# Four transformer layers and a routed expert layer on one core: joining the masks of two block pairs, moving bulk loads into the loop, preparing the experts' second group earlier

## The reference

```python
x = x + attn(layernorm(x))     # 4 layers inside
x = x + ffn(layernorm(x))      # experts
# attn: for each of 4 layers, h being the running state
xn = ln(h); q, k, v = xn @ Wq.T + bq, xn @ Wk.T + bk, xn @ Wv.T + bv     # 16 heads of 8
rel = einsum('bhqd,ld->bhql', q + u, pos_emb)
scores = (q k^T + rel_shift(rel)) * 8**-0.5; scores = where(k > q, NEG, scores)
h = h + softmax(scores) v @ Wo.T + bo
h = h + gelu(ln(h) @ W1.T + b1) @ W2.T + b2                              # 128 -> 512 -> 128
# ffn: a shared gated unit of width 256, and 16 experts of width 32
shared = silu(x @ sg.T) * (x @ su.T) @ sd.T
combine = weights of the top 4 of 16 experts, from the 2 best of 4 groups
routed = sum over e of (silu(x @ g_e) * (x @ u_e) * combine_e) @ d_e
```

## Time and profile before

| | |
|---|---|
| runs | 2417.66, 2413.36, 2417.36 us, median 2417.36 |
| profiled execution | 2418.66 us; its span 2416.9 us |
| granted TensorE clock, mean | 0.985 of full |
| instructions | 83238 |

### The profile page before, as it was taken

How to read it: one execution, slowest core, us unless ns; L and a number is a source line. 1 busy time by engine, 2 the same in 40 slices (tenths; PEclk the granted TensorE clock), 3 DMA queues, 4 the chain that set the end, 5 groups by cost and what they waited for, 6 DMA issues and landing times. The chain is left out here.

```text
span 2416.9 us, 83238 instructions
## 1 busy us (share of the span) xinstructions
PE 2301.1 (95%) x31360; PEld 1983.0 (82%) x31360; DVE 2020.7 (84%) x5071; ACT 1832.1 (76%) x2869; POOL 1145.7 (47%) x2089
## 2 busy tenths in 40 slices
PE   3899999999999999999999999999999999799998
PEld 2788888888888888888888888888888887577776
DVE  6899999888888888888888888888888885577774
ACT  2588888888888888888888888888878888455554
POOL 4355555455555544545555555454445543233332
PEclk9899999999999999999999999999999999699999
DMA  6333333333333333333333333333333330000000
GB/s 195 91 81 88 95 88 88 85 87 89 90 91 96 91 89 88 90 92 82 90 89 95 90 92 91 91 85 91 92 95 91 91 92 26 24 27 27 27 23 18
DMA packets 221160, 196.05 MB, mean 81 GB/s; under 512 B 28896, under 2 KB 217440, under 8 KB 220768
## 3 DMA queue, kind: packets, MB, share of 16 engines
q1 hardware_dynamic: 220768, 190.73, 29.2%
HBM read 14.46 MB, written 4.19 MB: 8 GB/s over the span
## 5 line engine op out<-in xcount | busy, mean ns | idle before, releaser
L961 DVE TENSOR_REDUCE rowmax<-bank 128x4 f32<-128x1024 f32 (+1 forms) x768 | 914.2, 1218 | 108.5 <-PE bank L556 96.4
L766 ACT ACTIVATE probs<-bank 128x1024 f32<-128x1024 f32 x768 | 745.7, 1024 | 89.2 <-PE bank L613 77.1
L613 PE MATMUL bank<-qstack,kstack 64*128 64x128 f32 (+1 forms) x4096 | 433.3, 304 | 0.0
L556 PE MATMUL bank<-kstack,qstack 62*128 62x256 f32 (+1 forms) x4096 | 427.1, 305 | 0.0
L807 ACT ACT_TABLE_LOAD x256 | 328.4, 1283 | 4.5
L556 PEld LDWEIGHTS bank<-kstack,qstack 62*128 62x128 f32 x4096 | 315.6, 193 | 0.0
L613 PEld LDWEIGHTS bank<-qstack,kstack 64*128 64x128 f32 x4096 | 314.8, 191 | 0.0
L545 PE MATMUL bank<-mask_half,pick_half 64*128 64x128 bf16 (+1 forms) x3072 | 269.6, 243 | 16.1 <-DMA qstack<-base 13.7
L602 PE MATMUL bank<-maskT_half,pick_half 64*128 64x128 bf16 (+1 forms) x3072 | 268.8, 241 | 15.2 <-DVE rowmax L961 10.5
L698 PE MATMUL bank<-w,hidden 128*128 128x128 f32 x2048 | 274.6, 278 | 2.6 <-ACT hidden L816 2.6
L633 PE MATMUL bank<-probs,v_pad 128*32 128x256 f32 x4096 | 271.1, 382 | 0.6 <-DVE v_tok L942 0.6
(11 more groups left out here) (151 smaller groups left out, 5261.8 us busy)
## 6 DMA issues: line engine op xcount, KB each, us to landing
qstack<-base SPq DMA_DIRECT2D x768, 128.0 KB, 2.4
kstack<-base SPq DMA_DIRECT2D x384, 128.0 KB, 2.5
turn_x<-turn_c SPq DMA_DIRECT2D x512, 32.0 KB, 1.8
qstack<-maxrows SPq DMA_DIRECT2D x256, 16.0 KB
out<-ot SPq DMA_DIRECT2D x16, 256.0 KB, 2.4
xin<-in_x SPq DMA_DIRECT2D x15, 256.0 KB, 3.1
w<-in_w SPq DMA_DIRECT2D x4, 256.0 KB, 3.1
w_in<-in_w_in SPq DMA_DIRECT2D x1, 768.0 KB, 4.3
```

What stands on the lines that cost most here:

```text
L556: last = pe.matmul(bank[:, b0 + b, i * wide:(i + 1) * wide], qstack[rows, r, p0 + i, t * 128:(t + 1) * 128], kstack[rows, r, p0 + i, 0:wid ...
L613: last = pe.matmul(bank[:, b0 + b, i * wide:(i + 1) * wide], kstack[rows, r, p0 + i, kt * 128:(kt + 1) * 128], qstack[rows, r, p0 + i, q0: ...
L766: act.activation(probs[:, k], bank[:, A_BANK[k]:A_BANK[k] + 2, :], ACT.Exp, scale=SCALE).then_inc(exp_done[k], 1)
L961: dve.tensor_reduce(rowmax[:, n % 2, t, :, p0:p0 + heads], bank[:, M_BANK[k]:M_BANK[k] + 2, :].rearrange("p b (h c) -> p b h c", h=heads), ...
```

## The change

Four things are moved; no product and no transfer is added or dropped, but the second group's residual now reads its x through `turn`, a tile that no one uses any more by then.

1. **Masks.** `m_round` is split into `m_masks` and `m_scores`, `a_round` into `a_masks` and `a_scores`. For most rounds they are called one after the other. At two places of a slot, a1 with m2 and m5 with a0, both masks come first and both sets of scores behind them. The wait of m5 for its stacks and of a5 for `maxrows` now stands at the scores.
2. **Bulk loads.** They move from SP's start into slots, each behind `exchange`: x rows 3 in slot 1, b_o, w_1, w_o in slot 2, b_2, b_1, w_2 in slot 3, x rows 4 and 5 in slots 4 and 8, w_qkv of layers 1 to 3 in slot 10. POOL splits `w_1` in slot 3 instead of slot 1.
3. **POOL in the drain.** The power of the experts' group 0 moves from the end of slot 131 to slot 132, behind `xn2_split`.
4. **Second group.** Its x is loaded in slot 129, its residual and statistics are made by DVE in slot 132, its power by POOL in slot 133, its norm as the first thing of DVE in the slots of the expert part (`norm(1)`).

```diff
@@ sync
-            sp.dma_start(w_1[:], a["w_1"][0]).then_inc(w1_landed, 16)
-            sp.dma_start(b_o[:], on_all("bo")).then_inc(later_landed, 16)
...
-            for c in range(3, len(X_STARTS)):
-                rows_of_x(c)
-            sp.dma_start(w_qkv[:, 1:LAYERS], a["w_qkv"].rearrange("l p n -> p l n")[:, 1:LAYERS]).then_inc(later_landed, 16)
+
+            def loads_behind(s):
+
+                if s == 1:
+                    rows_of_x(3)
+                if s == 2:
+                    sp.dma_start(b_o[:], on_all("bo")).then_inc(later_landed, 16)
+                    sp.dma_start(w_1[:], a["w_1"][0]).then_inc(w1_landed, 16)
+                    sp.dma_start(w_o[:], a["w_o"].rearrange("l p n -> p l n")).then_inc(later_landed, 16)
+                if s == 3:
...
+                    sp.dma_start(w_2[:], a["w_2"].rearrange("l (c p) n -> p l c n", p=128)).then_inc(later_landed, 16)
+                if s in (4, 8):
+                    rows_of_x(3 + s // 4)
+                if s == 10:
+                    sp.dma_start(w_qkv[:, 1:LAYERS], a["w_qkv"].rearrange("l p n -> p l n")[:, 1:LAYERS]
+                                 ).then_inc(w_rest_landed, 16)
+            def experts_second():
+
+                sp.wait_ge(cosines_used, N)
+                sp.dma_start(turn[:].rearrange("p b (t d) -> p b t d", t=T), x_tiles[:, GT // T:2 * GT // T]
+                             ).then_inc(ex.second_landed, 16)
@@ tensor, the slot's order
-                    a_round(s - 4, 1)
+                    a_masks(s - 4, 1)
                 if live(s - 2):
-                    m_round(s - 2, 2)
+                    m_masks(s - 2, 2)
                 if live(s - 4):
-                    a_round(s - 4, 4)
+                    a_scores(s - 4, 1)
                 if live(s - 2):
-                    m_round(s - 2, 1)
+                    m_scores(s - 2, 2)
...
                 if live(s - 1):
-                    m_round(s - 1, 5)
+                    m_masks(s - 1, 5)
                 if live(s - 3):
-                    a_round(s - 3, 0)
+                    a_masks(s - 3, 0)
+                if live(s - 1):
+                    m_scores(s - 1, 5)
                 if live(s - 3):
-                    a_round(s - 3, 3)
+                    a_scores(s - 3, 0)
@@ vector
+            def experts_stats_second():
+                h = h_all[:, 2:4].rearrange("p b t d -> p (b t) d")
+                dve.wait_ge(ex.second_landed, 16)
+                dve.wait_ge(h2_ready, N - B + 4)
+                dve.tensor_tensor(h, turn[:].rearrange("p b (t d) -> p (b t) d", t=T), h, ALU.add).then_inc(ex.x1_ready, 1)
...
                 if s == N + 4:
                     experts_norm()
+                    experts_stats_second()
@@ gpsimd
+                if s in (N + 4, N + 5):
+                    g = s - N - 3
+                    pool.wait_ge(ex.mv_ready, g)
+                    pool.tensor_scalar(ex.ve[:], ex.mv[:, :, 1], 1e-5, None, ALU.add).then_inc(ex.ve_ready, 1)
+                    pool.wait_ge(ex.ve_ready, g)
+                    at_least(pool, ex.xn_ready, g - 1)
+                    pool.tensor_tensor(ex.rstd[:], ex.ve[:], expo[:, 0:GT], ALU.pow).then_inc(ex.rstd_ready, 1)
...
-                if s == N + 3:
-                    pool.wait_ge(ex.mv_ready, 1)
@@ experts, vector
-                    if u == 1 and live(q + 2) and q + 2 > 0:
+                    if u == 1 and live(q + 2) and q + 2 > 1:
                         residual(q + 2, v + 2)
...
+            norm(1)
             slots(dve, slot)
```

More of the change, by code:

```diff
@@ L179 @@
     landed: object
+    second_landed: object
     x1_ready: object
@@ L513, in values, with m_mask, m_masks @@
                 last.then_inc(v_done, 1)
[L515 to L520, removed]
+            def m_mask(k, half):
+                heads = 4 if k < 2 else 2
+                for b in range(TILES):
+                    rows = slice(b * ROWS, (b + 1) * ROWS)
+                    v = bank[:, M_BANK[k] + b, :].rearrange("p (h k) -> p h k", h=heads)
+                    c = (0 if k < 2 else 128) + half * 64
+                    pe.matmul(v[:, :, c:c + 64], pick_half[rows, half], mask_half[rows, half, 0:heads],
+                              start=(half == 0), stop=True, skip_group_check=True)
+            def m_masks(n, k):
                 if k == 0:
@@ L536, in m_round, with m_scores @@
                     bank_left(pe, (live(n - 3), context_out, n - 2), (live(n + 1), v_ready, n + 2))
+                m_mask(k, 0)
+                if k >= 2:
+                    m_mask(k, 1)
+            def m_scores(n, k):
+                r, b0 = n % RING, M_BANK[k]
+                if k == M_FIRST:
+                    pe.wait_ge(stack_landed[r], 16 * STACK_DMAS * (n // RING + 1))
+                    pe.wait_ge(rot_landed[r], 16 * NP * (n // RING + 1))
                 t, heads = (0, 4) if k < 2 else (1, 2)
                 p0, wide = heads * (k - 2 * t), 512 // heads
[L540 to L550 removed]
                 for i in range(heads):
                     if heads == 4 and i == 1:
[L553 removed]
+                        m_mask(k, 1)
                     for b in range(TILES):
@@ L569, in m1, with a_mask, a_masks @@
                 last.then_inc(max_turned, 1)
-            def a_round(n, k):
-                r, b0 = n % RING, A_BANK[k]
-                if k == A_FIRST:
-                    pe.wait_ge(maxrows_landed, 32 * (n + 1))
+            def a_mask(k, half):
+                heads = 2 if k % 3 < 2 else 4
+                for b in range(TILES):
+                    rows = slice(b * ROWS, (b + 1) * ROWS)
+                    v = bank[:, A_BANK[k] + b, :].rearrange("p (h q) -> p h q", h=heads)
+                    c = half * 64
+                    pe.matmul(v[:, :, c:c + 64], pick_half[rows, 2 + half], maskT_half[rows, half, 0:heads],
+                              start=(half == 0), stop=True, skip_group_check=True)
+            def a_masks(n, k):
                 if k == 0:
@@ L595, in a_round @@
                 p0, wide = 4 * half + (2 * kind if kind < 2 else 0), 512 // heads
-                def mask(part):
-                    for b in range(TILES):
-                        rows = slice(b * ROWS, (b + 1) * ROWS)
-                        v = bank[:, b0 + b, :].rearrange("p (h q) -> p h q", h=heads)
-                        c = part * 64
-                        pe.matmul(v[:, :, c:c + 64], pick_half[rows, 2 + part], maskT_half[rows, part, 0:heads],
-                                  start=(part == 0), stop=True, skip_group_check=True)
-                mask(0)
-                if heads == 2:
-                    mask(1)
                 for i in range(heads):
                     if heads == 4 and i == 1:
-                        mask(1)
+                        a_mask(k, 1)
                     for b in range(TILES):
@@ L1330, in load @@
                     sp.dma_start(xin[:, v % 2], x_groups[q]).then_inc(xin_landed[v % 2], 16)
-            load(1, 1)
             def slot(q, v):
```

84 lines of the change are left out of this document (56 added, 28 removed).

## The result

The changed kernel takes 2404.88 us, the median of 5 runs (2402.57 to 2405.32), against 2417.25 us (5 runs) for the kernel before on the same chip: a ratio of 0.9949, 95% interval 0.9938 to 0.9961. I had predicted 2401.5 us. The profiled executions are 2418.66 and 2404.88 us with spans of 2416.9 and 2403.1: 13.8 us came in where I had summed 15.8. The joins, the drain and the expert part brought more than worked out, and the start had the wrong sign. That these offset each other is luck, and without it the sum would have been far off.

What follows compares the result with a forecast made beforehand. A slot was bound by a cycle of PE stretches and waits for DVE's maxima. Terms 6.2 + 2.0 + 2.7 + 4.9 = 15.8 us off 2418.66 gave 2402.9, less 1.3 to the median: 2401.5 us, range 2391 to 2411.

Steps and rivals of the forecast that it cites:

- Joined masks: In the slots: joining a1 and m2 saves 0.05 us in about 124 slots, 6.2 us; joining m5 and a0 saves 0.
- a2 waiting for the delayed exponential: In the slot, ahead of the wait at `f2`: a2's mask may wait up to 0.1 us; counted as nothing.
- The start, first half: At the start: with the loads moved away, the first exchange and content come sooner, 7.0 us saved.
- The start, second half: In slots 1 to 10: the six moved loads cost 5.0 us, leaving 2.0 us of the start's gain.
- The rate: Bulk loads in the slots: at 238 GB/s 1.05 MB of x takes 4.4 us, part of it while SP issues.
- The room: Before `split_first`: 3.0 us to spare in slot 8; no feed-forward hangs on ACT in slots 1 to 4.
- The sign that I had named: In slots 4 to 10: the clock falling behind a load would show the prediction wrong; no size given.
- the far bound: For one moved load in the slots: the worst row, `experts_early`, lost 5.0 us; bounds were 0 and 5.0.
- The drain: In slot 132: POOL splits item 126 ahead of the experts' power, so the split comes 2.7 us sooner.
- the clock comes back sooner: Rival for drain and expert part: products leave the half clock level earlier, 8 us more, 2393.5 us; chance 0.16.
- The expert part: At the second `x_turn`: PE's wait for the second group's norm goes away, 4.9 us saved.
- slower, each load costs 5.0: Rival for the moved loads: late stacks hold ACT and the clock falls, 30 us instead of 5, 2426.5 us; chance 0.05.

Runs made afterwards that it cites:

- no_joins: The changed kernel with both joins taken apart, each round's masks right ahead of its scores again: 2415.19 us, ratio 0.9998 to the kernel before the change.
- m2_scores_first: m2's scores put ahead of a1's, against the changed kernel with bulk and early loads ahead of the exchange (2388.59 us): 2400.26 us.
- before: The kernel without the change, against which the ratios are taken: 2417.25 us beside the changed kernel.
- after: The changed kernel as profiled, with all four moves, against the kernel without them: 2404.88 us, ratio 0.9949.
- loads_on_act_queue: The changed kernel with the bulk loads of slots 1, 2, 3, 4, 8 and 10 issued by ACT on its own queue instead of SP: 2392.98 us.
- pool_order_old: The changed kernel with the power of the experts' group 0 back at slot 131's end on POOL, ahead of item 126's split: 2410.64 us.
- second_group_old: The changed kernel with the second group's x, residual, statistics and norm back in the expert part: 2408.72 us, ratio 0.9977.
- loads_at_start: The changed kernel with its bulk loads back at the start of SP's queue, ahead of the first exchange: 2398.13 us, ratio 0.9921.

## Why the prediction was nearly right in sum and wrong in a term

- **Joined masks: right, 7.3 us instead of 6.2** (6.4 and 0.9 in the table; 7.5 to slot 127 by `no_joins`). Mechanism and place held: the join ahead of m2's end pays, the one under m0's maximum doesn't, and a third one ahead of `f2` doesn't. The term was sized from starts rounded to 0.01 us (0.84 against 0.78), and I took the low end, 0.05; the slots give 0.062 to 0.069. That the order is worth nothing, as I read the Trainium skill's rule on early weight loads (page "TensorE: Matmul & The Clock Gate", section "Step-by-step: what each phase is for"), is not borne out: the order alone is worth 0.07 us a slot here. Whether it is a weight load that stays exposed, and which, no run shows. What I counted at nothing, a2 waiting for the delayed exponential, was 0.02 us a slot; `m2_scores_first` shows how near that edge is.
- **The start, first half: right, 7.9 us instead of 7.0.** SP issues the exchange at 21.34 and the second `split_first` comes at 29.71. Ahead of it stood ten loads, not nine; no number hangs on that.
- **The start, second half: wrong.** "I take 1 us for each of five and 0 for the last" failed; only the 0 for slot 10 and the 1 for slot 3 came true. Slots 2 to 10 lost 16.0 us, with 4.4, 4.1, 3.9 and 2.7 us behind the loads of slots 1, 2, 4 and 8. Two steps of it were off.
  - The rate: I took 238 GB/s from the start and let part of the load go while SP still issues; in slot 8 the last content transfer is issued 1.9 us later behind `values` than in before (12.3 against 10.4) and lands 6.0 us behind its issue instead of 2.5, so the megabyte of x set it back by some 5.4 us, 195 GB/s, with nothing hidden. Against 3.0 us to spare that gives 2.4, and ACT is 2.4 us later (2.6 us behind `values` instead of 0.2).
  - The room: I thought that slots 1 to 4 had more of it since no feed-forward hangs on ACT there. The sum that gave 3.0 us for slot 8 (last issue plus 2.5 us, against the next `split_first`) gives in before 0.0, 2.4, 2.9 and 0.5 us for slots 1 to 4, an estimate: the two loads of x in slots 1 and 4 met next to no room. Why slot 2 lost 4.1 us with 2.4 to spare stays open.

  The sign that I had named came true as well: the clock fell behind a load in slots 4 to 10. The nearest row was `experts_early`, and I had kept it as the far bound.

  The rule named there, that the descriptors of one ring are consumed in order (the Trainium skill, page "DMA: Bandwidth & Descriptors", section "Queues, rings and completion order"), agrees with slot 8 of after, where the content lands behind the load; the page also says that a later descriptor may finish its write before an earlier one, so "waits for all of it" was my own step. It explains half of the loss: on another queue (`loads_on_act_queue`) the other half stays.
- **The drain: the wait right, 2.7; its consequence left out.** The stretch gained 6.7. PE no longer idles 4.66 us, and item 126's products run at full clock, `up` in 2.02 us instead of 3.75 (the granted clock is 0.70 instead of 0.51 from 2060 to 2080); item 127's `up` runs at half in both. `pool_order_old` puts 5.4 us on this one order on POOL, and the means of all kernels 6.2. I had this as a rival ("the clock comes back sooner", 8 us, chance 0.16) and not in the sum.
- **The expert part: right, 6.3 instead of 4.9.** The second `x_turn` follows the first group's first product, and `second_group_old` gives 5.0 us for it; the other 1.3 appear in the profile of before alone, where the half level lasted longest (the clock is 0.58 from 2080 to 2100, 0.96 in after).
- **The slot behind the early load** gained 1.7 us that no part of the change is for. In seven kernels with that load at the same place it is 17.2 to 20.1 us, in before 20.44; why it varies stays open.

Of the rivals, "slower, each load costs 5.0" had the right mechanism (late stacks hold ACT, PE idles, the clock falls) and half of its size: 14.5 to 16 us for six loads against its 30. The other terms kept the total out of its reach.

## What to carry to other kernels

In this pipeline a bulk transfer costs what it puts behind it. Place it where its queue is idle and the next urgent transfer is the farthest away, not right ahead of the pipeline's own transfers; moving these loads and the early one by 5.5 us within the slot was worth more than the whole change (0.9885 against 0.9949). Price such a load by the worst place where the trace already shows it, and subtract room only where a row of the same slot shows room.

Engine time that is saved under or right ahead of a wait for another engine paid nothing here (the joins of m5 with a0 and of m3 with m4), and each order has several such waits: before a swap, list what each moved instruction reads, the bank that it writes, and who used that bank last.

Where an engine idles for some us in a drain, count the wait twice: once for itself and once for the products behind it at the half clock, 2.7 and 3.5 us here. Then compare several kernels of the same drain, since one alone is uncertain by up to 5 us.

## What the runs showed of the hardware

- Two groups of bf16 mask products and two of f32r scores take 0.77 us joined and 0.84 us alternating; the first scores behind masks take 0.32 us, scores behind scores 0.24.
- 1.05 MB of x ahead of 0.77 MB of stacks in one queue set them back by some 5.4 us (slot 8 of after). Beside them on ACT's queue a stack transfer still took 5.3 us to land instead of 2.5, but was issued on time.
- With the same drain program the clock falls at different places. In after it is at half from 2064.5 us, 74 us behind `values` of slot 127, in `no_joins` twice, 66 and 76 us behind it, and in `loads_at_start` only behind the first `x_turn`. The first `x_turn` comes 78.7 to 84.1 us after `values` of slot 127. A change of up to 5 us at the end of one profile is within what this alone does.
